# Issuing the transpose of the last x2 tile from ScalarE instead of SyncE, in a one-core graph transformer layer

## The reference

```python
xn = layernorm(x)
x1 = x + gnn(xn, src, dst) + linear_attention(xn)     # two SAGE layers, one attention
h  = gelu(bitlinear(layernorm(x1), w1))               # w1: 4096 x 1024
out = x1 + bitlinear(h, w2)                           # w2: 1024 x 4096

def bitlinear(x, w):     # activations rounded to 8 bits by row, weights to -1, 0, 1
    return quant_act(x) @ quant_weight(w).T
```

## Time and profile before

| | us |
|---|---|
| median of 3 runs (lowest, highest) | 1363.65 (1363.03, 1364.96) |
| the profiled execution, its own time | 1363.81 |
| its span, first to last instruction | 1362.0 |
| TensorE matmuls busy | 1334.5 (98%) |
| VectorE busy | 870.6 (64%) |
| ScalarE busy | 463.1 (34%) |

### The profile page before, as it was taken

The page is one execution under the profiler, slowest core; times in us unless marked ns, Lnnn a source line. Parts: engine busy times, 40 slices in busy tenths (PEclk is TensorE's granted clock), DMA queues, the critical chain, the costliest instruction groups (busy, mean ns, idle before and its releaser), DMA issues.

```text
span 1362.0 us, 20063 instructions
## 1 busy us (share of the span) xinstructions
PE 1334.5 (98%) x6642; PEld 632.5 (46%) x6642; DVE 870.6 (64%) x1511; ACT 463.1 (34%) x672; POOL 3.8 (0%) x16
## 2 busy tenths in 40 slices
PE   8999999999999999999999999999999997999998
PEld 5445445555444544444444444444444443444443
DVE  6835452352677865655879958845876575876773
ACT  6655664354311222221111112200000175464450
POOL 0000000000000000000000000000000000000000
PEclk9989999999999999999999999999999999999999
DMA  8296887764135441104676764645544529414523
GB/s 340 69 302 212 282 280 231 268 235 164 69 109 186 154 158 46 32 1 129 196 200 185 204 196 140 231 155 192 181 159 147 155 47 278 99 53 98 124 58 97
DMA packets 172911, 219.97 MB, mean 162 GB/s; under 512 B 93857, under 2 KB 127137, under 8 KB 171553
## 3 DMA queue, kind: packets, MB, share of 16 engines
q1 hardware_dynamic: 128480, 207.95, 46.5%
q10 hardware_dynamic: 44352, 11.02, 4.8%
HBM read 164.41 MB, written 32.51 MB: 145 GB/s over the span
## 4 chain that ended last, share of the span: by engine, by line
PE 88%; DVE 4%; DMA 3%; issue 2%; ACT 2%; DVEq 0%; ACTq 0%; POOL 0%; POOLq 0%
PE ps L1653 51%; PE ps L1891 12%; PE ps L1772 7%; PE ps L1978 6%; PE ps L2015 6%; PE ps L1837 3%; DMA XH<-HL 1%; PE ps L1697 1%; DMA AT<-Zb 1%; PE ps L1679 1%; PE ps L1780 1%; DVE Zb L1470 1%; ACT Zb L838 1%; PE ps L1728 0%; DVE AM L1493 0%
## 5 line engine op out<-in xcount | busy, mean ns | idle before, releaser
L1653 PE MATMUL ps<-S,XH 128*128 128x512 f16 x2400 | 528.3, 380 | 1.7 <-DVE TMP L1012 1.4
L1653 PEld LDWEIGHTS ps<-S,XH 128*128 128x128 f16 (+1 forms) x2400 | 233.1, 98 | 279.4 <-issue 2.1
L1891 PE MATMUL ps<-Zb,AT 128*128 128x512 f16 x800 | 177.0, 381 | 0.0
L1891 PEld LDWEIGHTS ps<-Zb,AT 128*128 (+1 forms) x800 | 78.5, 98 | 95.4 <-issue 2.2
L1653 PE MATMUL ps<-S,Zb 128*128 128x512 f16 x480 | 106.3, 379 | 0.0
L1772 PE MATMUL ps<-XH,S 128*128 128x512 f16 (+1 forms) x576 | 102.6, 339 | 0.0
L1223 DVE TENSOR_SCALAR STREAM<-tables,keys 128x320 f16 x240 | 72.4, 302 | 43.0 <-issue 31.2
L1653 PE MATMUL ps<-Zb,XH 128*128 128x512 f16 x432 | 96.4, 383 | 0.0
L1328 DVE SCALAR_TENSOR_TENSOR STREAM<-STREAM,cols 128x1024 fp8e4<-128x1024 f32 x64 | 79.2, 1279 | 0.0
L1772 PEld LDWEIGHTS ps<-XH,S 128*128 128x128 f16 x576 | 56.1, 98 | 47.0 <-issue 2.3
L741 ACT ACTIVATE AT<-ps 128x320 f16<-128x320 f32 x40 | 17.5, 438 | 163.8 <-PE ps L1842 163.8
(11 more groups left out here) (237 smaller groups left out, 1412.4 us busy)
## 6 DMA issues: line engine op xcount, KB each, us to landing
STREAM<-in_w1t SPq DMA_DIRECT2D x64, 512.0 KB, 5.1
STREAM<-in_w2t SPq DMA_DIRECT2D x52, 512.0 KB, 4.4
STREAM<-in_w_all SPq DMA_DIRECT2D x48, 512.0 KB, 5.8
XIN<-in_x SPq DMA_DIRECT2D x20, 512.0 KB, 5.2
SPLIT<-in_Wneigh SPq DMA_DIRECT2D x16, 512.0 KB, 6.0
SPLIT<-in_Wself SPq DMA_DIRECT2D x16, 512.0 KB, 4.5
w1q_scratch<-STREAM SPq DMA_DIRECT2D x16, 512.0 KB, 5.0
w2q_scratch<-STREAM SPq DMA_DIRECT2D x16, 512.0 KB, 3.6
```

Source lines behind the costliest of these rows:

```text
L1653: last = mm(acc[:, n * BANK:(n + 1) * BANK], left(l, kc), right(kc, r)[:, n * BANK:(n + 1) * BANK], start=(kc == 0 and i == 0), stop=(kc = ...
L1891: last = mm(banks(bank + n, 1), AT_tile(t, s), Z[:, r, s, n * BANK:(n + 1) * BANK], start=(s == 0 and r == 0), stop=(s == NT - 1 and r == 1))
```

## The change

ScalarE issues the transpose of tile 9 in the first half of f1(1), between the Gelus of step 2 and those of step 3. Before it, ScalarE waits until the transposes of SyncE that came before (hidden rows of pair 0, tile 8) have landed, and for the rounded rows of tile 9. SyncE no longer issues it; it waits for it to have landed before its first transpose of pair 1.

```diff
             sp.dma_start(S1[:, 8 * D:12 * D], w2q_d[:, 16 * D:20 * D]).then_inc(S("w2_T1_in"), 16)
             sp.dma_start(S1[:, 4 * D:8 * D], w2q_d[:, 12 * D:16 * D]).then_inc(S("w2_B22_in"), 16)
-            x2T_turn(9, 1)
             sp.wait_ge(S("x1_out"), 16 * NT)
...
                 if more:
+                    if p == 0:
+                        sp.wait_ge(*x2T_in(9, 1))
                     hid_turn(2 * p + 2, 0, 1)
...
-            def f1_act(p, g, after_copies=(), after_first=()):
+            def f1_act(p, g, after_copies=(), after_first=(), after_gelus=()):
...
                     gelu(t, 1, 2 * g + s, F1_BANKS[s][0])
+                for step in after_gelus:
+                    step()
                 for s in range(2):
...
-            f1_act(1, 0, [lambda: y_round(9)], [lambda: y_std(9)])
+
+            def x2T_last():
+                for half in range(2):
+                    act.wait_ge(S(f"gT{half}"), 32)
+                act.wait_ge(*x2T_in(8, 0))
+                x2T_act(9, 1)
+
+            f1_act(1, 0, [lambda: y_round(9)], [lambda: y_std(9)], [x2T_last])
```

## The result

The changed kernel takes 1364.91 us (median of 19 runs, 1361.15 to 1372.63), the kernel before 1362.21 us (19 runs, 1358.59 to 1366.31). The ratio is 1.0023, with a 95% interval of 1.0012 to 1.0034: slower. The ratio makes this 3.1 us (1.6 to 4.6 by its interval), the two medians differ by 2.7 us.

A forecast was written before the change was run, and what follows sets the result against it. TensorE, busy 98% of the span, was the bound, so only its gaps could move: landing 2.8 us later plus 0.2 us more low clock, +3.0 us, median 1366.65 us; likeliest case 1365.4 to 1368.0, 8 in 10 1361.0 to 1368.5.

The forecast's parts named there:

- The place that decides: Landing of tile 9's transpose, moved from q1 to q10: forecast 2.8 us later, with TensorE restarting 3.26 us after it.
- gap and clock: TensorE's 5.9 us wait for VectorE's sum before 1156.19, plus 2.1 us lost to the low clock behind it: 8.0 us.
- Equal turns: DMA engines alternate q1 and q10 packet by packet, read from 170 to 173.5 us: 364 packets against 363.
- the landing near 1145: Alternative landing if one turn moved 16 pieces of 256 bytes against one of 8 KB: four turns would do.
- The landing time: Transpose issued at 1140.65, first packet near 1142.4, some 46 turns, last 18 packets alone: lands 1155.7 (1154.7 to 1156.5).
- the end of the traffic stays where it was: Total bytes unchanged, so DMA traffic still ends with the second x1 load, which landed at 1155.6 before.
- The clock: Low clock behind TensorE's longer gap lasts between nothing and 1.7 us more, taken as 0.2.
- The pause on ScalarE: ScalarE's 1.9 us issue pauses TensorE about 1.2 us (0.5 to 1.9) at 1143, hidden while the sums' wait remains.
- B: Rival, chance 0.20: the transpose gets through early, before 1152.9; gap and clock go, gain 5.9 us, time 1357.75.
- C: Rival, chance 0.15: transpose done before the x1 loads, landing within 1 us of 1152.9; time 1363.7.
- D: Rival, chance 0.05: ScalarE is held in the issue, up to 6.01 us, shifting f1(1) by 5 us; time 1368.5.
- The chances in the prediction: Summed over the forecast and rivals, with 0.2% (2.7 us) as threshold: faster 0.19, same 0.40, slower 0.41.

The follow-up runs named there:

- e3: Kernel before, SyncE issuing: rows of tile 9 lie in a free half of TMP, so the first block sum need not wait for the transpose; ratio 0.9947.
- e4: Changed kernel, ScalarE issuing: rows of tile 9 lie in a free half of TMP, so the first block sum need not wait; ratio 0.9947.
- e5: Changed kernel, but SyncE waits for tile 9's transpose to land before issuing the last two weight blocks and both x1 loads; ratio 0.9953.
- e7: Kernel before, but SyncE issues tile 9's transpose ahead of the six weight blocks, with the store of x1 moved to the front; ratio 0.995.
- e6: Changed kernel, store of x1 moved to the front; SyncE waits for tile 9's transpose to land before issuing any of six weight blocks; ratio 0.9984.
- e1: Changed kernel, but each of the six weight blocks SyncE loads is cut into four transfers of 2 KB per partition; ratio 1.0001.

## Why the prediction was right, point by point

**The place that decides.** "This is what decides" was the landing of the transpose, and it did. Nearly all of the measured difference (2.7 of 2.96 us in the traces) is in the gap before 1156.39 and the low clock behind it; e3 and e4, which take the wait away and leave the late landing, gain 7.2 us. That also sizes gap and clock: the forecast's 8.0 us, less 0.8 us, which is what TensorE's wait of 0.76 us for VectorE in e3 would account for.

**Equal turns.** Read off one stretch early in the kernel with packets of 4 KB and carried over to packets of 8 KB. Shown: 279 to 304 in the changed kernel, 548 to 551 with 2 KB packets. That a turn might move 16 small pieces against one of 8 KB, which the wording of the Trainium skill (DMA: Bandwidth & Descriptors, Queues, rings and completion order) leaves open, is not what these counts show, and the landing near 1145 did not come. The rule of the same page that DMAs of any issuing engine share the 16 engines and interleave (Issuing engines are not separate DMA queues) agrees with the trace: 95.2% and 7.3% of the engines' time side by side.

**The landing time.** The forecast was 15.05 us after the issue (1155.7 less 1140.65), measured 14.86. But the terms behind it were mis-sized, and they partly cancel. The first packet was to go 1.75 us after the issue; it went after 4.2 to 4.4. From there to 1151.2 us, where q1 was nearly through, q10 had 597 of its packets, 37 for each engine and not 46, and the rest, 29 for each engine and not 18, went at the end (q10 has 1056 packets here, 32 more than the forecast counted):

```profile
q10 hardware_dynamic: 459, 0.11, 26.8%
q1 hardware_dynamic: 34, 0.09, 11.3%
```

(1151.2 to 1153.2 us). This tail took over a microsecond, not 0.3 to 0.4 us, and the transpose landed 0.4 us behind the second load of x1, not 0.1. And "the end of the traffic stays where it was" was not quite so. From the issue of the last weight block to the landing of the second load of x1 it was 21.6 us before (1134.0 to 1155.6) and 20.6 us after (1132.15 to 1152.7, which is 1144.7 and 8.0 us of landing):

```profile
L494 SPq DMA_DIRECT2D XIN<-x_scratch x1: 433/433/433, 1144.7 to 1144.7; - x1
...
DMA to landing us min/median/max: 8.0/8.0/8.0
```

So q1 ended 1.0 us earlier than forecast and the transpose 0.3 us later behind it. The late first packet did not count, because the end of q1 set the landing. Where the 1.0 us was saved is argued, not shown by a run: before, the transpose stood in q1, and the engines moved little meanwhile (this row is of the kernel before, 1149.5 to 1151.5 us):

```profile
DMA packets 533, 0.28 MB, mean 142 GB/s; under 512 B 514, under 2 KB 514, under 8 KB 514
```

In the changed kernel, the stretch from 1149 to 1151 us moves 358 GB/s. So the landing moved by 2.05 us, where 2.8 was forecast. VectorE's wait grew by less, to 8.8 us and not to the 10 that the forecast named, because VectorE came to it some 0.4 us later as well.

**The clock.** Forecast: between nothing and 1.7 us more, taken as 0.2. It was 0.6. With the landing this makes 2.7 us against the forecast's 3.0: 0.7 us too much on the landing and 0.4 too little on the clock. The measured difference is known only to 1.6 to 4.6 us, so the agreement of 3.0 with it to a few tenths is luck; what is borne out is the mechanism and the size within some 1.5 us.

**The pause on ScalarE.** Forecast 1.2 us (0.5 to 1.9), hidden as long as the wait remains. It was hidden, and it is 0.3 us when uncovered. The issue's length was nearly right (1.57 us, forecast 1.9), but it was taken to start when the Gelu ends. The timeline has it start 0.15 us after the Gelu's start, so that 0.54 us of it lies beside the Gelu. With that the forecast's own account closes: 1.57 less 0.54, less the 0.4 us that ScalarE had stood idle and the 0.3 us that the copy had been early, leaves 0.3 us.

**The rivals.** B (faster by 5.9 us) had the right price for an early landing: e5 and e7 land early and gain 6.4 and 6.8 us. Its condition, that q1 leaves the engines room, was not met. C did not come: the loads of x1 left no pause. D did not come: the issue took 1.57 us, not 6. The chances in the prediction are added up wrongly by 0.01: its terms give 0.18 faster and 0.41 the same.

**Left open.** Why the first packet of q10 goes some 4 us after the issue where q1 is full, against 1.1 us alone (e6), was not tried by itself; cutting the packets from 8 to 2 KB shortened it only from 4.2 to 4.4 us to 3.8 to 4.0. Nor is it settled why e4's landing took 17.9 us, 3 us more than in the changed kernel. Its trace shows where: from 1152 to 1159 us both queues had work, and the engines moved 91 GB/s in all.

```profile
q1 hardware_dynamic: 122, 0.47, 62.9%
q10 hardware_dynamic: 672, 0.16, 52.5%
```

This execution was the slowest of e4's five (1359.11 us, the median 1354.95), so it may not be typical; nobody waited for the transpose.

## What to carry to other kernels

In these runs a transpose with packets of 256 bytes did not overtake loads with packets of 8 KB by going on another queue: it got one packet for each packet of the other, and was through about when the other queue ran empty. Beside packets of 2 KB it was through earlier, but by less than the counts promised (e1). What helps is order, by issuing it ahead of the bulk (e7, 0.995) or holding the bulk back behind it (e5, 0.9953), or removing the reason why somebody waits (e3, 0.9947). Holding back everything costs at the other end, where the last load of the bulk becomes late (e6).

## What the runs showed of the hardware that was not expected

A transpose issued on an idle queue beside a full one moved no packet for 4.2 us (changed kernel, 8 KB packets beside it) and 3.8 us (e1, 2 KB packets); with nothing beside it, for 1.1 us (e6). A DMA issue on ScalarE overlaps the activation in front of it: it started 0.15 us after the start of a Gelu of 0.69 us, in the changed kernel and in e4.
